# A fused attention and feed-forward layer: accumulating DMAs for the sums of two bidirectional gates, and other places for their scans

## The reference

```python
tf    = sigmoid(sum(time_emb, -1))
decay = exp(-exp(w)) * (0.5 + 0.5 * tf)
ek    = exp(min(k, 30)); ekv = ek * v            # here v is k too
nf, df = forward scans  a = a * decay + (ekv, ek)
nb, db = the same scans backward in time
euk   = exp(min(u + k, 30))
num   = nf + nb - ekv + euk * v
den   = df + db - ek + euk
gate(r) = sigmoid(r) * (num / max(den, 1e-8)) * (0.8 + 0.2 * tf)

x = x + attention(gate1(x))        # 16 heads of 16, causal softmax, with biases
x = x + ffn(gate2(x))              # ffn: down(silu(up(x)) * gate(x)), hidden size 1024,
                                   # the three weights quantized to {-1, 0, 1} * scale
```

## Time and profile before

| | |
|---|---|
| median of three runs | 182.76 us (182.74 to 183.18) |
| the profiled execution | 182.91 us, span 181.1 us |
| DVE busy | 156.2 us, 86%, 262 instructions |
| PE busy | 147.6 us, 82%, 1544 matmuls |
| ACT busy | 114.7 us, 63% |
| POOL busy | 51.1 us, 28% |
| mean granted clock of PE | 0.981 |
| normalize(0), (1), (2) on DVE start at | 57.38, 96.26, 132.97 us |

### The profile page before, as it was taken

One profiled execution on the slowest core, in us unless ns is written; L12 is line 12 of the kernel. 1 busy time (PEld: TensorE's weight loads), 2 busy tenths in 40 slices (PEclk: granted clock), 3 DMA queues, 4 the chain that ended last, 5 costly groups with the idle time before them and its releaser, 6 DMA issues. The chain is left out here.

```text
span 181.1 us, 3815 instructions
## 1 busy us (share of the span) xinstructions
PE 147.6 (82%) x1544; PEld 97.6 (54%) x1544; DVE 156.2 (86%) x262; ACT 114.7 (63%) x181; POOL 51.1 (28%) x49
## 2 busy tenths in 40 slices
PE   0008597973999889999899689997998999997991
PEld 0008483331348656764576357744764676785880
DVE  0699958999999979999998999999769999986672
ACT  2638756999777743589357634883593348885550
POOL 8700032999700049340000194400002223000000
PEclk9999789999699999999999999999999999999999
DMA  4999204000000400000132000000420000010001
GB/s 100 360 430 424 108 29 145 4 0 2 0 5 0 173 5 0 0 5 0 58 103 76 0 4 0 2 4 4 144 87 0 0 5 4 4 62 2 4 0 58
DMA packets 5706, 10.91 MB, mean 60 GB/s; under 512 B 760, under 2 KB 4024, under 8 KB 5304
## 3 DMA queue, kind: packets, MB, share of 16 engines
q1 hardware_dynamic: 5400, 10.52, 15.4%
q10 hardware_dynamic: 288, 0.14, 0.5%
HBM read 6.43 MB, written 1.05 MB: 41 GB/s over the span
## 5 line engine op out<-in xcount | busy, mean ns | idle before, releaser
L245 POOL TENSOR_TENSOR extra<-extra,k_t 128x512 f32<-128x512 f32 x7 | 8.9, 1268 | 84.3 <-DVE fwd L589 40.9
L676 DVE TENSOR_REDUCE row_max<-wide 128x4 f32<-128x1024 f32 (+1 forms) x24 | 28.8, 1216 | 0.6 <-PE wide L1039 0.6
L437 ACT ACTIVATE silu<-attn_ps,up_scale 128x256 f32<-128x256 f32 x24 | 11.2, 473 | 24.6 <-PE attn_ps L986 22.1
L399 ACT ACTIVATE probs<-wide 128x1024 f32<-128x1024 f32 x24 | 23.9, 1020 | 3.2 <-PE wide L1064 2.6
L589 DVE TENSOR_TENSOR_SCAN fwd<-decay,ek 128x256 f32<-128x256 f32 x32 | 21.1, 704 | 0.0
L601 DVE TENSOR_TENSOR_SCAN bwd<-ek,decay 128x255 f32<-128x255 f32 x32 | 21.1, 706 | 0.0
L270 POOL TENSOR_TENSOR hid_lo<-hid,hid_hi 128x512 f16<-128x512 f32 x9 | 12.4, 1380 | 14.3 <-ACT hid_hi L444 14.3
L1184 PE MATMUL wide<-ones 128*128 128x128 f32 x24 | 4.5, 369 | 14.1 <-DVE fwd L776 14.1
L986 PE MATMUL attn_ps<-x_lo,w_tern 128*128 128x256 f16 x96 | 13.9, 273 | 1.2 <-DVE x_lo L701 1.2
L986 PE MATMUL attn_ps<-x_hi,w_tern 128*128 128x256 f16 x96 | 14.3, 274 | 0.0
L1034 PE MATMUL wide<-mask_qk,identity_b 128*128 128x256 bf16 (+1 forms) x48 | 11.0, 311 | 3.6 <-DMA stack<-halves 1.9
(11 more groups left out here) (144 smaller groups left out, 343.3 us busy)
## 6 DMA issues: line engine op xcount, KB each, us to landing
stack<-halves SPq DMA_DIRECT2D x24, 128.0 KB, 2.1
w_raw<-wup_d SPq DMA_DIRECT2D x1, 1024.0 KB, 11.5
w_raw<-wgate_d SPq DMA_DIRECT2D x1, 1024.0 KB, 13.2
w_raw<-wdown_d SPq DMA_DIRECT2D x1, 1024.0 KB, 15.0
out_d<-x_t SPq DMA_DIRECT2D x4, 256.0 KB, 2.3
wqkv<-wqkv_d SPq DMA_DIRECT2D x1, 768.0 KB, 7.2
k_t<-k_d SPq DMA_DIRECT2D x1, 768.0 KB, 8.6
x_t<-x_d SPq DMA_DIRECT2D x1, 768.0 KB, 10.0
```

Source lines behind the costliest of these rows:

```text
L399: nc.scalar.activation(probs[:, j, :], flat(wide[j % 2][:, :, :]), ACT.Exp, scale=SOFTMAX_SCALE).then_inc(prob_done, 1)
L437: nc.scalar.activation(silu[:, e % 2], up, ACT.Silu, scale=up_scale[:, 0:1]).then_inc(silu_done, 1)
L676: nc.vector.tensor_reduce(out, src, AX.X, ALU.max).then_inc(max_done, 1)
```

## The change

- **Sums.** For gate one, batches 2 and 3, and for gate two, batches 0 to 2, both sums become DMAs issued by POOL that add to their destination: `send_extra` (fwd += extra) and `send_backward` (fwd += bwd), each 128x1024 f32, with a semaphore for each kind and gate. That is ten DMAs. Readers wait by `wait_extra_added` and `wait_summed`. Gate one of batches 0 and 1 and gate two of batch 3 keep their sums on DVE.
- **Scans.** All gate one scans of batches 2 and 3 stand at the end of the turn before, one tile of them after `normalize`. Gate two's forward scans of batches 1 and 2 go ahead of its backward scans. Batch 3's backward scans of gate two stand around `normalize(2)`, its forward scans between gates 5 and 7.
- **Order.** `refine(1, f)` comes after `normalize(f)`, `second_wkv(f)` after `residual(f)`; `first_reciprocal(1, f)` after `row_reciprocals(f)`. `bound_denominator(1, b)` comes between the low halves.
- **Feed-forward input.** DVE writes the f32 input by tiles, ACT copies the high part (`high_input`), DVE subtracts (`low_input`).
- **Start.** POOL forms both products of batch 0; one gain row and two decay rows follow `first_gate(0)`; PE has three more warm-up matmuls after the second reciprocal product. ACT does `minus_maxima(0)` after the first ternary pass, `key_exp(3)` after `exp_probs(0, 3)`, and the ternary pass of the down weights in turn 1.
- **Turn 1 on PE.** Two up_gate parts stand ahead of `scores(1, 0)`.
- **Tail.** `tail_low` and `tail_halves` split the last group by tile.

```diff
+        def by_dma(c, b):
+            return b >= 2 if c == 0 else b < B - 1
+        def wait_summed(engine, c, b):
+            if by_dma(c, b):
+                engine.wait_ge(sum_in[c], 16 * (b - 1 if c == 0 else b + 1))
+            else:
+                engine.wait_ge(sum_done[c], b + 1 if c == 0 else 1)
...
-            def add_extra(c, b):
+            def send_extra(c, b):
                 pool.wait_ge(prod_done[c], b + 1)
                 pool.wait_ge(fwd_done[c], 4 * b + 4)
-                nc.gpsimd.tensor_tensor(fwd[c][:, :, :], fwd[c][:, :, :], extra[c][:, :, :],
-                                        ALU.add).then_inc(fwd_extra[c], 1)
+                pool.dma_start(fwd[c][:, :, :], extra[c][:, :, :], accum_op=ALU.add).then_inc(extra_in[c], 16)
+            def send_backward(c, b):
+                wait_extra_added(pool, c, b)
+                pool.wait_ge(bwd_done[c], 4 * b + 4)
+                pool.dma_start(fwd[c][:, :, :], bwd[c][:, :, :], accum_op=ALU.add).then_inc(sum_in[c], 16)
...
             nc.gpsimd.memset(ones_pad[:, PAIR:PAIR + HD], 0.0).then_inc(v_ones, 1)
+            values_of_keys(0)
+            extra_products(0, 0)
...
             extra_products(0, 1)
+            send_extra(1, 0)
             bound_keys()
             pool.wait_ge(vec_in, 16)
             bound_sums(1)
+            send_backward(1, 0)
             bound_sums(0)
             values_of_keys(2)
             for b in range(1, B):
                 more = b + 1 < B
+                pool.wait_ge(x2lo_done, b)
                 if more:
-                    if b == 1:
-                        pool.wait_ge(x2lo_done, b)
-                    pool.wait_ge(fwd_done[0], 4 * b + 8)
                     extra_products(0, b + 1)
-                    add_extra(0, b + 1)
-                else:
-                    pool.wait_ge(x2lo_done, b)
+                    send_extra(0, b + 1)
                 extra_products(1, b)
                 low_hidden(b - 1, 0)
                 if b + 2 < B:
                     values_of_keys(b + 2)
                 low_hidden(b - 1, 1)
+                if more:
+                    send_backward(0, b + 1)
                 low_hidden(b - 1, 2)
+                if more:
+                    send_extra(1, b)
+                    send_backward(1, b)
...
+            def high_input(b):
+                for ct in range(CT):
+                    act.wait_ge(x2_done, 2 * b + ct + 1)
+                    nc.scalar.activation(x2_hi[:, ct, :], x2[:, ct * T:(ct + 1) * T],
+                                         ACT.Copy).then_inc(x2hi_done, 1)
...
                     if b > 1:
-                        first_product(1, f)
                         normalize(f)
-                        second_product(1, f)
+                        if more:
+                            backward(0, b + 1, 0, (1,))
+                        else:
+                            backward(1, b, 1, (1,))
+                            backward(1, b, 0)
+                        refine(1, f)
+                    residual(f)
+                    if b > 1:
                         second_wkv(f)
-                    residual(f)
                     ffn_input(f)
-                    if more:
-                        forward(0, b + 1, 0)
+                    low_input(f)
...
                     last_halves(f)
+                    bound_denominator(0, b + 1)
+                    forward(1, b, 1)
+                    forward(1, b, 0)
+                    refine(0, b + 1)
+                    gate_first(b + 1)
+                    first_wkv(b + 1)
+                    backward(1, b, 1)
+                    backward(1, b, 0)
+                    finish(f)
                     if b + 2 < B:
                         forward(0, b + 2, 1)
+                        forward(0, b + 2, 0)
+                    low_halves(b + 1, 1)
                     if b + 2 < B:
                         backward(0, b + 2, 1)
+                    bound_denominator(1, b)
+                    low_halves(b + 1, 0)
+                    if b + 2 < B:
+                        backward(0, b + 2, 0, (0,))
+                    else:
+                        backward(1, b + 1, 1, (0,))
...
-                    add_extra(1, 0)
-                    sums(1, 0)
                     bound_denominator(1, 0)
                     dve.wait_ge(scale_done, 4)
                     dve.wait_ge(bo_done, 1)
-                    forward(0, 2, 1)
-                    backward(0, 2, 1)
+                    for half in (1, 0):
+                        forward(0, 2, half)
+                    for half in (1, 0):
+                        backward(0, 2, half)
...
+            pe.wait_ge(recn_done[0], 1)
+            for _ in range(3):
+                nc.tensor.matmul(wide[0][:, 0, 0:P], ones[:, :], ones[:, :], start=True, stop=True)
...
+                    if b == 1:
+                        up_gate(f, 0, 0)
+                        up_gate(f, 1, 0)
                     scores(b, 0)
                     scores(b, 1)
-                    for part in range(2):
+                    for part in range(b == 1, 2):
                         up_gate(f, 0, part)
                         up_gate(f, 1, part)
```

More of the change, by code:

```diff
@@ L125, in build @@
         w_in = [sem(f"w_in{i}") for i in range(3)]
+        extra_in, sum_in = ([sem(f"{n}{c}") for c in range(2)] for n in ("extra_in", "sum_in"))
         k_top_done, roundneg_made = sem("k_top_done"), sem("roundneg_made")
@@ L581, in scan_ready, with forward @@
                     dve.wait_ge(ekv_done, b + 1)
-            def forward(c, b, half):
+            def forward(c, b, half, tiles=range(CT)):
                 if b:
@@ L586, in forward @@
                 scan_ready(b, half)
-                for ct in range(CT):
+                for ct in tiles:
                     d = decay[:, 2 * c + ct, b, :].broadcast_to([P, T])
@@ L591, in forward, with backward @@
                                                  ALU.mult, ALU.add).then_inc(fwd_done[c], 1)
-            def backward(c, b, half):
+            def backward(c, b, half, tiles=range(CT)):
                 if b:
-                    dve.wait_ge(sum_done[c], b)
+                    wait_summed(dve, c, b - 1)
                 scan_ready(b, half)
-                for ct in range(CT):
+                for ct in tiles:
                     d = decay[:, 2 * c + ct, b, :].broadcast_to([P, T - 1])
@@ L844, in _ @@
                     gate(f, 5)
-                    if more:
-                        backward(0, b + 1, 0)
-                    else:
-                        backward(1, b, 1)
+                    if not more:
+                        forward(1, b, 1)
                     gate(f, 6)
-                    if more:
-                        sums(0, b + 1)
-                    else:
-                        backward(1, b, 0)
+                    if not more:
+                        forward(1, b, 0)
@@ L854, in _ @@
                     gate(f, 7)
                     last_halves(f)
-                    if more:
-                        bound_denominator(0, b + 1)
-                        backward(1, b, 1)
-                        backward(1, b, 0)
-                    forward(1, b, 1)
-                    if more:
-                        refine(0, b + 1)
-                        gate_first(b + 1)
-                        first_wkv(b + 1)
-                    forward(1, b, 0)
-                    if more:
-                        finish(f)
@@ L923, in _ @@
             tail_input(1)
-            for g in range(NG):
-                for e in range(EG):
-                    gate(f, EG * g + e)
-                    if e == 0 and g:
-                        dve.wait_ge(hidhi_done, (NG - 1) * f + g)
-                        if g >= 3:
-                            dve.wait_ge(down_done, NG * f + g - 2)
-                        nc.vector.tensor_tensor(hid_lo[:, (g - 1) % 2], hid[:, (g - 1) % 2], hid_hi[:, (g - 1) % 2],
-                                                ALU.subtract).then_inc(hidlo_done, 1)
-            last_halves(f)
+            for e in range(ET):
+                g = e // EG
+                gate(f, e)
+                if e % EG == 0 and g:
+                    tail_low(g - 1)
+                if g == NG - 1:
+                    tail_halves(e)
             finish(f)
@@ L1008, in down @@
                     for e in range(EG):
+                        if g == NG - 1 and b == B - 1:
+                            pe.wait_ge(last_hi if half is hid_hi else last_lo, B + e)
                         for dt in range(CT):
```

86 lines of the change are left out of this document (53 added, 33 removed).

## The result

| | median us | lowest to highest | executions |
|---|---|---|---|
| before | 182.34 | 180.78 to 184.38 | 20 |
| changed | 183.50 | 182.16 to 184.57 | 20 |

The ratio is 1.0074 [1.0043, 1.0104]: the change makes the kernel about 1.35 us slower by that ratio (1.16 by the medians), where 5.2 us of gain were forecast. Ratios leave out executions in a second, slower state; the profiled ones of b1_warm (191.83 us) and e4_halves (185.28) are of that kind. The profiled execution of the changed kernel took 182.16 us (span 180.4), 0.75 less than the profiled one of before; that pair of traces alone would have given the wrong sign.

A forecast was written before the change was run, and what follows sets the result against it. DVE was taken to bound the start and both ends of a turn, PE and ACT its middle. The terms summed to -5.2 from the profiled 182.91 us: 177.7, or 177.5 as median, range 176.0 to 179.0 with chance 0.48.

The forecast's parts named there:

- Start, -1.0: Before the first wkv: two products moved to POOL (-0.65), gain and decay rows out of the chain (-0.35).
- Clock, -1.6: First keys on PE: three more warm-up matmuls keep 2.4 GHz, so they take 2.00 us in place of 3.65.
- the keys stay slow: Rival: the first keys stay at 1.2 GHz despite the added matmuls, ending at 179.1; chance 0.12.
- Turn 0, -0.15: Turn 0 on DVE: two sums of gate two leave (-2.5), two scan pairs come in (2.35).
- Feed-forward input, -0.3 and +0.2: One DVE pass fewer brings x_lo 0.3 earlier; ACT before silu comes 3.0 earlier where 3.2 were due, +0.2.
- `row_max` in turn 2, -1.15: Start of turn 2: without the scan pair before the maxima, PE's 1.25 us wait shrinks to 0.1.
- `wkv` waits, -1.85: End of turns 1 and 2: wkv is ready before PE's weighs end, so waits of 0.91 and 0.93 go.
- The DMA pair: Loss 2(L - 5.7) + (2L - 10.2) + (2L - 10.0), positive terms only; at landing time L = 4.8 us, 0.
- Turn 3, +1.0: Turn 3's head: refine behind backward scans puts residual 3.67 after normalize; with second_wkv, 1.0 us more on the path.
- PE's waits stay: Rival: PE's waits at wkv and row_max stay because DVE's list runs over; 3.0 lost, 180.5; chance 0.15.
- slow DMAs: Rival: accumulating DMAs land slowly; L above 6.15 eats the whole gain, at 7 the time is 188; chance 0.14.
- Issues stretched by DVE: Rival: DVE stretches POOL's DMA issues, L becomes 6.0, loss 4.4, ending at 181.9; chance 0.08.

The follow-up runs named there:

- b1_warm: The kernel before with only three more warm-up matmuls, waiting for the second reciprocal product: 0.9998 of before.
- e4_halves: The changed kernel with gate two's two DMAs split into 256 KB halves, denominator first, in all three batches: 1.0115 of before.
- b2_before: The kernel before, unchanged, run a third time for its trace: 181.01 us.
- c0_after: The changed kernel run again as it is: 1.0075 of before, its traced execution 182.08 us.
- b0_before: The kernel before, unchanged, run once more for a second trace: 181.72 us.
- e3_start: The changed kernel with the two products of batch 0 back on VectorE: 1.0029 of before.
- experiment 4: The runs on the start, e3_start (1.0029 of before) and b1_warm (0.9998), with VectorE rows of the changed kernel.
- e1_small: The changed kernel with each of the ten DMAs moving only 128x8 elements (output wrong, time only): 179.99 us, 0.9911 of before.
- e5_turn3: The changed kernel with turn 3's refine and residual right after normalize, backward scans among the gates, forward scans near the end: 1.0000 of before.
- e7_sum0: The changed kernel with gate one's backward sum of batches 2 and 3 back on VectorE, between gates 6 and 7: 1.0123 of before.
- e11_best2: The changed kernel with e3_start's and e5_turn3's edits, gate two's backward sum on VectorE, and e7_sum0's edit: 179.18 us, 0.9841 of before.
- e2_early: The changed kernel with gate one's second DMA issued ahead of low_hidden(b-1, 0): 1.027 of before.

## Why the prediction was wrong

The sum stood against one execution of before. Set against b2_before, which is one of its short executions (181.01), with c0_after (182.08), from normalize to normalize:

| stretch | forecast | b2_before | c0_after | difference |
|---|---|---|---|---|
| to first wkv | -1.0 | 19.52 | 19.68 | +0.2 |
| to normalize(0) | -1.75 | 35.91 | 36.33 | +0.4 |
| turn 1 | about -1.2 | 38.93 | 39.05 | +0.1 |
| turn 2 | about -2.2 | 36.72 | 35.80 | -0.9 |
| to the end of the span | +1.0 | 48.12 | 49.34 | +1.2 |

The forecast fell short in four places: the DMAs (counted as 0, they cost 3.0 us), the low clock of the first keys (1.6 that most of the runs had no need of), the start (1.0), and turn 3, where its cost was right and a fall of the clock came on top. The turns themselves went as told: with small DMAs turns 1 and 2 are 1.46 and 1.80 shorter than in b2_before, 3.3 together against about 3.4 forecast, and the bytes take 2.5 of it. The other trace of before with fast keys, b0_before, has 36.30 and 39.24 in the second and third line, so only the +1.2 and the -0.9 of the table are clear of what differs between traces of one kernel (and, within turn 0, the 0.6 up to wkv(1) below).

- **Start, -1.0: failed.** Nothing came of it: the first scan is 0.2 to 0.8 later behind the exponential than before. POOL's products beside the chain stretch it by more than they save. That they were "hidden" was argued for the scans that read them and never for the small VectorE steps they run beside. e3_start and the rows of experiment 4 show it.
- **Clock, -1.6: failed as a gain.** The step took 3.65 us from the one trace. The mechanism (keys at 2.4 GHz) came as told and the trace pair shows it, maxima from 30.08 instead of 31.71; but two other traces of before have it already, and b1_warm, which has this part alone, gains nothing (0.9998). The 0.12 given to "the keys stay slow" asked the wrong question: whether the changed kernel would be fast there, not whether the old one always was slow.
- **Turn 0, -0.15 and the rest: +0.4.** From the last of the maxima to wkv(1) VectorE takes 12.98 us instead of 12.36 (from the first wkv 30.01 instead of 29.39, and 29.38 in b0_before). POOL's stream is two issues longer (1.01 and 0.91 us in c0_after), so `uk_top` and values_of_keys(2) run beside other VectorE instructions; in both kernels single ones are stretched (`gate_first` to 1.76 in c0_after, the first product to 1.65 in b2_before, each 0.7 elsewhere), in the changed one for 0.6 more in sum. From wkv(1) to normalize(0) it is 0.2 shorter, as forecast. The reading of the traces is all there is for this; no run took it apart.
- **Feed-forward input, -0.3 and +0.2:** x_lo ends 6.39 after normalize(0) instead of 7.01; that is -0.6, more than forecast, but the maxima of turn 1 then wait 1.03 for PE.
- **`row_max` in turn 2, -1.15: came.** Maxima follow x_lo at once, and it is the one gain that is left: turn 2 is 0.9 shorter.
- **`wkv` waits, -1.85: gone, and eaten by others.** DVE's `wkv` is early enough (84.27 against PE's keys at 85.26), but PE reaches its keys late by the new `neg_max` wait, and turn 1 ends on something else.
- **The DMA pair: the term that failed most.** L was 4.4 to 4.5 alone against 4.8 forecast, and an issue 0.85 to 1.0 us against 1.0. The loss formula used one L for every DMA. Gate two's second DMA is issued (87.16 in the first trace) beside the output transfer and the stack's, and took 6.3 in turn 1 (4.9 in turn 2 in much the same company; why these differ was not found). The formula also let the second DMA start when the first had landed. In the trace it waits for the backward scans, which end at 86.45 in c0_after, and POOL picks the issue up 0.55 us later; VectorE was ready for the bound at 91.38, 4.4 behind the issue. So of the slack of 10.2, which was right, only 4.4 was the second DMA's: its forecast 4.8 would have cost 0.4, and its 6.3 cost 1.96. Behind it normalize(1) stood 1.1 later than `row_rec` allowed, where the sum had 0. The other side of the same step was missed whole: not what the DMAs wait for but who waits behind them. The 8 KB `neg_max` transfer took 3.31 us behind a DMA of 512 KB, against at most 2.46 in turn 1 of b2_before (issue 73.99, scores at 76.45), at most 2.46 with small DMAs, and 1.85 in turn 0 of b2_before. Together the bytes cost 3.0 us (e1_small).
- **Turn 3, +1.0: right in size** (residual 3.67 after normalize as forecast, e5_turn3 0.9 in the trace), and incomplete: it leaves PE idle for 1.80 us instead of 0.62, and in three of ten traces the clock falls behind that, for 1.1 us more.

Of the rivals, "PE's waits stay" (180.5) named the right loss, gains at `wkv` that don't arrive, but both of its waits went and others came; "slow DMAs" had the sign, by a size of L (over 6.15) that only the slowest of the ten reached. "Issues stretched by DVE" did not happen. The prediction's estimate of 4.4 us rests on the Trainium skill ("Collectives: The Full Stack", the bandwidth ceiling: the add costs a second source read). It agrees with the medians of 4.4 and 4.5, and it told nothing of a transfer in company, 6.3 us.

## What to carry to other kernels

Work that goes from a busy engine to a DMA has three prices that its own duration doesn't show: the small transfers behind it, its length beside others, and the clock of TensorE if something waits. Put one trace of the kernel before beside a second before a gain is read from one stretch of it: what a single execution shows at a low clock may be no one's to win. And a fix that fails while another wait stands can work when that one is gone; try it again then (e7_sum0: 0.5% slower; in e11_best2 0.6% faster).

## What the runs showed of the hardware

- An accumulating DMA of 512 KB within SBUF takes 4.4 us alone. Beside an output transfer and the stack's it takes 6.3 to 7.1 in turn 1 and 4.9 to 5.3 in turn 2; one of 4 KB takes 2.0 alone, and 4.8 and 2.8 there (e1_small). A share of the loss is so not a matter of bytes.
- TensorE's granted clock fell to 0.50 during the projection behind 2.73 and 2.15 us of idle (e7_sum0, e2_early); it stayed at 1.00 behind 1.18 to 1.33 at the same place in the three traces of the changed kernel, and behind 1.56 in e3_start. With 2.12, 1.54 and 1.12 before the first keys it was low once, with the longest. With 1.80 at the head of turn 3 it fell in three traces of ten.
- TENSOR_SCALAR of 128x4 on VectorE took 0.97 us beside a GpSimd multiplication of two inputs, 0.17 without.
